# Four groups of four row blocks become groups of 3, 3, 3, 3 and 4

## The reference

```
lora_delta = lora_B @ lora_A * 0.5
normalized = (weight + lora_delta) / scale          # per 128 inputs
w_eff = codebook[searchsorted(thresholds, normalized)] * scale + lora_delta
y = x @ w_eff.T
result = y @ W_base.T + b_base
mixed = sum_e softmax(y @ router_w.T)_e * (y @ A_w.T) @ cores_e
out = x + result + (mixed @ B_w.T) * 2
```

## Time and profile before

| | |
|---|---|
| median of 3 runs | 2366.76 us |
| the profiled execution | 2369.28 us, span 2367.5 us |
| TensorE (PE) busy | 2288.2 us, 97% of the span |
| VectorE (DVE) busy | 1845.3 us, 78% |
| ScalarE (ACT) busy | 1462.2 us, 62% |
| GpSimd (POOL) busy | 1290.2 us, 54% |
| DMA | 459.62 MB, mean 194 GB/s |
| part to and from DRAM | 1036.0 KB each |
| x of one token tile, four blocks | 256.0 KB |

### The profile page before, as it was taken

The page is one execution under the profiler, slowest core; times in us unless marked ns, Lnnn a source line. Parts: engine busy times, 40 slices in busy tenths (PEclk is TensorE's granted clock), DMA queues, the critical chain, the costliest instruction groups (busy, mean ns, idle before and its releaser), DMA issues.

```text
span 2367.5 us, 31840 instructions
## 1 busy us (share of the span) xinstructions
PE 2288.2 (97%) x11778; PEld 2085.7 (88%) x11778; DVE 1845.3 (78%) x2360; ACT 1462.2 (62%) x1923; POOL 1290.2 (54%) x792
## 2 busy tenths in 40 slices
PE   3989999999999999999999999999999999999998
PEld 2444479999999999999999989999998999999998
DVE  8999988889978857777777966777775566766766
ACT  8999978889876646566646655566553554121121
POOL 6888836679763436767664436766652114233231
PEclk9999999999999999999999999999999999999999
DMA  6788854443334435676664335666665665656553
GB/s 209 276 286 285 313 183 172 155 166 143 139 139 123 118 109 195 229 233 238 229 214 144 117 98 183 230 234 236 220 221 172 181 187 188 232 188 224 192 210 152
DMA packets 133087, 459.62 MB, mean 194 GB/s; under 512 B 14098, under 2 KB 66898, under 8 KB 96082
## 3 DMA queue, kind: packets, MB, share of 16 engines
q1 hardware_dynamic: 132932, 457.59, 56.9%
HBM read 306.41 MB, written 151.13 MB: 193 GB/s over the span
## 4 chain that ended last, share of the span: by engine, by line
PE 90%; DVE 4%; ACT 3%; DMA 2%; issue 1%; SPq 0%; DVEq 0%; ACTq 0%
PE m L949 15%; PE m L948 15%; PE m L950 15%; PE m L847 6%; PE m L905 5%; PE m L906 5%; PE m L904 5%; PE m L997 3%; PE m L999 3%; PE m L998 3%; PE m L935 2%; DVE acc L1339 2%; PE m L937 2%; PE m L936 2%; ACT mk L1110 1%; PE pd L997 1%
## 5 line engine op out<-in xcount | busy, mean ns | idle before, releaser
L1339 DVE SCALAR_TENSOR_TENSOR acc<-mk,dj,acc 128x1024 f32<-128x1024 uint8 x736 | 945.0, 1284 | 92.4 <-ACT mk L1110 71.9
L1110 ACT ACTIVATE mk<-wr,bj 128x1024 uint8<-128x1024 f32 x736 | 809.6, 1140 | 1.4 <-DVE acc L1339 1.0
L949 PE MATMUL m<-gl,xh 128*128 128x384 f32 (+2 forms) x1920 | 674.1, 351 | 0.0
L948 PE MATMUL m<-gh,xh 128*128 128x384 f32 (+2 forms) x1920 | 673.5, 351 | 0.0
L950 PE MATMUL m<-gh,xl 128*128 128x384 f32 (+2 forms) x1920 | 671.6, 350 | 0.0
L1583 POOL TENSOR_TENSOR pp<-pp,tm 128x1024 f32<-128x1024 f32 x184 | 447.5, 2432 | 22.3 <-POOL tm L1569 0.6
L950 PEld LDWEIGHTS m<-gh,xl 128*128 128x128 f32 x1920 | 360.6, 188 | 18.0
L948 PEld LDWEIGHTS m<-gh,xh 128*128 128x128 f32 x1920 | 361.0, 188 | 17.2
L949 PEld LDWEIGHTS m<-gl,xh 128*128 128x128 f32 x1920 | 360.9, 188 | 16.9
L1569 POOL TENSOR_SCALAR tm<-mp,dj 128x1024 f32<-128x1024 uint8 x192 | 217.9, 1135 | 279.7 <-ACT mp L1116 274.6
L1390 DVE TENSOR_TENSOR kl<-kw,kh 128x416 fp32r<-128x416 f32 (+3 forms) x312 | 240.1, 783 | 111.3 <-ACT kh L1144 110.3
(11 more groups left out here) (198 smaller groups left out, 3371.1 us busy)
## 6 DMA issues: line engine op xcount, KB each, us to landing
part<-part SPq DMA_DIRECT2D x192, 1036.0 KB, 7.6
rows<-in_wb SPq DMA_DIRECT2D x61, 1036.0 KB, 4.8
out<-part SPq DMA_DIRECT2D x31, 1024.0 KB, 4.5
kw<-in_ws SPq DMA_DIRECT2D x128, 208.0 KB, 2.6
xw<-in_x SPq DMA_DIRECT2D x96, 256.0 KB, 3.3
kw<-in_wb SPq DMA_DIRECT2D x92, 192.0 KB, 2.4
wr<-in_w SPq DMA_DIRECT2D x32, 512.0 KB, 8.7
dl<-delta SPq DMA_DIRECT2D x30, 512.0 KB, 6.0
```

What stands on the lines that cost most here:

```text
L948: e.matmul(R.m[c][:, 0:w], xh, gh, start=k == 0, stop=False)
L949: e.matmul(R.m[c][:, 0:w], xh, gl, start=False, stop=False)
L1110: e.activation(R.mk[m % NM], w, ACT.Identity, bias=R.bj[:, j:j + 1], scale=GROW).then_inc(S["mk"], 1)
L1339: e.scalar_tensor_tensor(R.acc, R.mk[m % NM], R.dj[:, j:j + 1], R.acc, ALU.mult, ALU.add).then_inc(S["ac"], 1)
```

## The change

GROUP becomes (3, 3, 3, 3, 4). There are four groups of three blocks, so there is one more G stage and one more token stage, and each of the first four token stages has 3 matmuls for 3 blocks per chunk. The shares of the background (UNTIL_TOKENS, UNTIL_WEIGHTS) are set for the new stages. From half block 2 * N0 = 6 on, a delta unit stands at every second level (from 3), where it was every third (from 5), from half block 8 on. In token stage 0 the low part of x is made by GpSimd (as in the other stages), and no longer by VectorE. One buffer rh lies elsewhere.

In the last G stage the small DMAs move from the event ("split", 31) to slot 8; bs is made in four pieces at slots 40, 43, 56 and 59; the first pair's x is loaded at slot 94 and prepared at slots 104 and 121. In the last token stage `turn` of the pair's second tile comes one product later.

```diff
-GROUP = (4, 4, 4, 4)
+GROUP = (3, 3, 3, 3, 4)
-UNTIL_TOKENS, UNTIL_WEIGHTS = (16, 24, 32), (0, 18, 26, 32)
+UNTIL_TOKENS, UNTIL_WEIGHTS = (12, 19, 26, 32), (0, 14, 21, 28, 32)
+LOW_AT, PAIR_AT = (40, 43, 56, 59), (104, 121)
...
-        if s == NSL - 14:
+        if s == 8:
+            yield ("small_factors",)
+        if s in LOW_AT:
+            yield ("low_weights", LOW_AT.index(s))
+        if s == PAIR_AT[0]:
             yield ("pair_high", 0)
             yield ("pair_sums", 0)
-        if s == NSL - 8:
+        if s == PAIR_AT[1]:
             yield ("sums_high", 0)
             yield ("pair_low", 0)
...
-                 13: (("turn", b), ("sums_high", p + 1), ("pair_low", p + 1)), 15: (("mix", b), ("second", p, 0)),
+                 13: (("sums_high", p + 1), ("pair_low", p + 1)), 14: (("turn", b),), 15: (("mix", b), ("second", p, 0)),
...
-    late += [(q, j) for q in range(2 * N0, NQ) for j in range(5, NV, 3)]
+    late += [(q, j) for q in range(2 * N0, NQ) for j in range(3, NV, 2)]
...
-                if s == NSL - 24:
+                if s == PAIR_AT[0] - 10:
                     load_pair(0)
...
-        elif what == "split" and at[0] == NQ - 1:
+        elif what == "small_factors":
             e.wait_ge(S["bw0"], 1)
...
-    def low_weights():
-        e.wait_ge(S["bw"], 48)
...
+    def low_weights(k):
+        at = slice(512 * k, 512 * (k + 1))
+        if k == 0:
+            e.wait_ge(S["bw"], 48)
...
+        e.activation(R.bs[:, at], R.bw[0:96, at], ACT.Copy).then_inc(S["bshi"], 1)
...
-        elif what == "x_split" and at[0] == 0:
-            split_x(at[1])
...
-        elif what == "x_split" and at[0]:
+        elif what == "x_split":
             split_x(*at)
```

More of the change, by code:

```diff
@@ L267, in __init__ @@
         self.fl[2:2] = [self.gh[N0 - 1], self.gl[N0 - 1]]
-        self.rh = [self.put(f"rh{k}", raw[0] + 4 * DX * k, DX, F32R) for k in range(3)]
+        self.rh = [self.put(f"rh{k}", at, DX, F32R) for k, at in enumerate((raw[0], raw[0] + 4 * DX, raw[2 * N0 + 2]))]
         at_k = [at_p[HOME[r]] + (r % 2) * 4096 for r in range(RING)]
@@ L1005, in prod @@
                 if p == 0:
-                    e.wait_ge(S["bs"], 1)
+                    e.wait_ge(S["bs"], 4)
             done = e.matmul(bank, R.sa[t % 3], R.bs[:, c0:c1], start=False, stop=True, skip_group_check=n == 4)
@@ L1170, in evacuate @@
         e.activation(R.part[t % 3][:, cols(c)], R.m[c][:, 0:width(c)], ACT.Copy).then_inc(S["ea"], 1)
-    def low_weights():
-        e.wait_ge(S["bw"], 48)
[L1174 to L1177, removed]
+    def low_weights(k):
+        at = slice(512 * k, 512 * (k + 1))
+        if k == 0:
+            e.wait_ge(S["bw"], 48)
+            e.wait_ge(S["bb"], 32)
+            e.wait_ge(S["cl"], NQ)
+            e.wait_ge(S["pp"], NA * NQ)
+        e.activation(R.bs[:, at], R.bw[0:96, at], ACT.Copy).then_inc(S["bshi"], 1)
     def copied(n, i):
@@ L1258, in scalar_program @@
                 weight(g, s + AHEAD)
-            if g == LAST and s == 20:
-                low_weights()
+        elif what == "low_weights":
+            low_weights(*at)
         elif what == "chunk_out":
@@ L1459, in weigh @@
                         p[:, D:D + NR].unsqueeze(1).to_broadcast([128, NE, NR]), ALU.mult).then_inc(S["z"], 1)
[L1461 to L1465, removed]
     def sharpen(t):
@@ L1511, in vector_program @@
         elif what == "split" and at[0] == NQ - 1:
-            wait_consumed(e, S, RAW * (NQ // RAW - 1) + 1)
+            wait_consumed(e, S, RAW * (NQ // RAW) + 1)
             e.memset(R.bw, 0.0).then_inc(S["bw0"], 1)
@@ L1519, in vector_program @@
                 weight(g, s + AHEAD)
[L1520 to L1523, removed]
+        elif what == "low_weights":
+            c = slice(512 * at[0], 512 * (at[0] + 1))
+            e.wait_ge(S["bshi"], at[0] + 1)
+            e.tensor_tensor(R.bs[64:96, c], R.bw[64:96, c], R.bs[64:96, c].bitcast(F32), ALU.subtract).then_inc(S["bs"], 1)
         elif what == "formed":
```

## The result

The changed kernel takes 2472.7 us (median; 2470.9 to 2485.2), against 2367.4 for the kernel before: ratio 1.0452, 95% interval 1.0432 to 1.0472. The profiled execution has a span of 2468.2 us. The forecast was 2460.

What follows compares the result with a forecast made beforehand. TensorE, busy 97%, was the bound; smaller groups would let VectorE hold G stages and stores hold token stages. -24.2 + 54 + 66 + 5 - 8 = +93 on 2369.3 us gave 2462, median 2460, range 2385 to 2550.

Steps and rivals of the forecast that it cites:

- TensorE's own sum: Whole kernel, if TensorE never waits: -72.8 us in the start-up, +45.4 G product, +3.2 delta units, sum -24.2 us.
- its other two terms: One more block's G product, +45.4 us, and eight more delta units in token stage 0, +3.2 us.
- token stage 0, and the handovers of stages 0 and 3: ScalarE's busier token stage 0 costs +3 us; less time for the last half block's wh and wl +2; sum +5.
- G stages of three blocks: VectorE becomes the bound in the first 48 slots, 88.7 us against 75.6: +18 us a stage, three times, +54.
- token stages 1 to 3: Loads and stores of partial sums hold each tile to 9.6 us against TensorE's 8.5: +22 us a stage, +66.
- companion's moves: Last G and token stages: fewer waits for kl and small gains from pair work and turn(b), -8 us, bounds 0 to -13.
- the chain of stores: Token stages 1 to 3: each load waits for an earlier store to land, the next store follows it; period 9.6 us.
- the formula: Length of token stages 1 to 3 at period P per tile: 34.4 + 27P, 293.6 us at 9.6, against 271.5.
- rival 2: Only the G stages are held; load and store land quicker, period at or below 8.9: +27 us, 2394 us, chance 0.22.

Runs made afterwards that it cites:

- The last experiment: Four groups with the companion's moves and store before load, 2357.1 us, against the changed kernel with store before load and one half block per three-block G stage, 2347.0 us.
- the store first: Changed kernel with the store of tile t-1 issued before the load of tile t+1 in SyncE's queue: 2383.5 us, ratio 1.0070 to the kernel before.
- half a store: Changed kernel storing only the first 1024 of 2072 columns of the partial sums in token stages 1 to 3: 2377.5 us.

## Why the prediction was right, step by step

| Step | predicted | measured |
|---|---|---|
| TensorE's own sum | -24.2 us | start-up with `final` 262.1 us (261.8 expected): -23.9, if its other two terms hold |
| token stage 0, and the handovers of stages 0 and 3 | +5 | +2.5 (288.4 against 285.9); stage 3's handover is in the row of the token stages |
| G stages of three blocks | 3 x 18 = +54 | +11.0, +18.3, +15.7 = +45 |
| token stages 1 to 3 | 3 x 22 = +66 | +26.7, +32.4, +30.4 = +89.5 |
| companion's moves | -8 | -12.4 (188.3 + 371.5 against 194.4 + 377.8) |
| span | +93 | +100.7 |

Both costs were there, with the causes that the prediction gave them. That the total came within 8 us is in part luck: the G stages cost 9 us less than I said, the companion's moves gave 4 more, token stage 0 took 2.5 less, and the token stages cost 23.5 more.

**TensorE's sum** held to 0.3 us in the start-up. The last experiment shows 10 us of it as a gain of the whole kernel.

**The G stages** are bound by VectorE, as the first 48 slots said: 88.7 us of work in 75.6. These slots (up to the first product of 512 columns) took 87.0, 94.2 and 92.3 us with VectorE 97% busy, and the other 32 slots 60.3, 60.4 and 59.7, where 3/4 of before is 60.8. So the whole loss stands where it was priced, and 75.6 + 18 = 93.6 is near two of the three. The light stages (-35 us for one half block less in each) agree, and the mean of L1397 rose from 0.95 to 1.02, 1.04 and 1.02, as a growing share of GpSimd wants. One thing was not in my text: TensorE's waits there stand mostly at gl (18.6 us), not kl (7.8), at the handover of finished chunks after 16, 32 and 48 slots, where I had looked at the splits alone. Another is not a wait: of the 45 us TensorE idled 27, and for the other 18 it was itself busy longer than 3 x 136.3, at a granted clock of 0.97 to 0.98.

The first G stage lost less than the other two. That is no property of the stage: with the store first, where the program is the same up to its end, it took 152.9 us instead of 147.3, and the mean of L1397 in it was 1.08 instead of 1.02 us, which is 5 us over its 76 instructions.

**The token stages** are bound by the chain of stores: periods 9.5, 9.7 and 9.5 us, predicted 9.6, each load issued as the store lands. The steps that moved the bound (the store first, half a store) released TensorE fully. With these periods the formula gives +20, +26 and +20, and the stages took 27, 32 and 30 more, 24 us more in sum. The term that was too small is the end of the stage: I gave the last adds 1.5 us, but the first loads of kw wait for the chain too, so TensorE waited 5.5, 4.8 and 9.8 us for the next stage. That is 16 us of the 24. The other 8 I can't place. A term that I had put at nothing is among the candidates: TensorE was busy 278.0 to 280.6 us in each stage, where with the store first it was busy 269.9 or 270.0, at a granted clock of 0.98 to 0.99, and no run separates the clock from the slower matmuls right behind a wait (0.44 us for 384 columns, elsewhere 0.34). The way by which the chain reaches TensorE (x late, ScalarE standing, masks late) I had not seen; x_split at chunk 4 shows that this way is not the cause.

The Trainium skill's fit ("DMA: Bandwidth & Descriptors", Anatomy of one DMA) would have made a period of 7.4 us, on the side of rival 2. The page gives it for DMAs issued by GpSimd, and these are issued by SyncE. The rows of the changed kernel disagree with it for a store behind a load: the store alone takes 8.6 us, where the fit has 6.9 for both (an estimate). They come nearer for a store that goes first: 4.9 us where the fit of the Trainium skill has 4.4 (an estimate from the same page, 2.0 us and 1.06 MB over 436 GB/s).

**Token stage 0** stayed out of trouble: ScalarE busy 261.7 us of 288.4 (predicted 265 of 286), and TensorE waited 3.2 us in all, 1.9 of it at the handover.

**The companion** gave 12.4 us in place, within my bounds of 0 to 13, and 10 by itself. The 3 us of SyncE's queue at slot 8 cost less than I feared: TensorE waited 2.5 us for kl in this stage, 6.5 before.

## What to carry to other kernels

When a change shrinks a stage's unit of work, list what each unit carries that does not shrink (here two transfers of partial sums, a low part per slot, quantization per stage), and compare each with the new unit, not with the mean busy share: the DMA engines were busy 66%, and the chain through them already took 9.4 us of a tile's 11.3. Two transfers that wait on each other through a ring of buffers make a period of their own; the order in which they are issued sets its length, and one line of order was worth 89 us here, and nothing with the longer tiles of four blocks. Follow a wait to what issues its cause: the longest wait of the profile (for x) led to late masks, and with the masks in time nothing was gained. Before explaining a difference of a few us between stages, look at the same stage in runs where nothing ahead of it was changed.

## What the runs showed of the hardware that I had not expected

- Order of issue between a 1036 KB load and a 1036 KB store on one queue (medians): load first, then store 0.5 us later, and the load lands in 6.5 us, the store in 8.6; store first, then load 0.4 us later, and the store lands in 4.9 us, the load in 7.7. Why the pair is quicker in this order no run tells.
- A 192 KB load issued behind them landed in 8.5 us (median), and in 3.0 us where it was issued ahead of them.
- The same traffic ran at 258 GB/s with the DMA share at 0.79, and at 286 GB/s with the share at 0.80, where TensorE never waited.
